# A state-space and FFN block: the scan's output is added to x by TensorE in the bank of y's transposes and copied by ScalarE, and SyncE's transfers are reordered

## The reference

```python
# 1: state-space block over the context, gated by the normalised x
u = silu(conv(in_proj @ ctx) + conv_b)
dt_lo, Bm, Cm = split(x_proj @ u);  delta = softplus(dt_proj @ dt_lo + dt_b)
state = state * exp(delta * A) + (delta * u) * Bm      # 512 steps, 16 states per channel
y = (sum_n state * Cm + D * u) * silu(layernorm(x))
x = x + tanh(g_xattn) * y^T
# 2: feed-forward block on layernorm(x): w1, w2 up (2048), w3 down
h = silu(bit_linear(r, w1, g1)) * bit_linear(r, w2, g2)
x = x + tanh(g_ffn) * bit_linear(h, w3, g3)
# bit_linear: rmsnorm, gain, rounding to 8 bits by the row's maximum, ternary weights
```

## Time and profile before

| | |
|---|---|
| median of the timed runs | 683.2 us |
| the profiled execution | 686.62 us |
| its span, first to last instruction | 684.7 us |
| busy: PE / DVE / ACT / POOL | 608.6 / 603.5 / 555.7 / 548.3 us |
| mean granted TensorE clock | 0.933 |
| DVE, scans of line 1272 | 128, 292.1 us |
| DVE, `add_input` of line 1263 | 128, 157.8 us |

### The profile page before, as it was taken

The page is one execution under the profiler, slowest core; times in us unless marked ns, Lnnn a source line. Parts: engine busy times, 40 slices in busy tenths (PEclk is TensorE's granted clock), DMA queues, the critical chain, the costliest instruction groups (busy, mean ns, idle before and its releaser), DMA issues.

```text
span 684.7 us, 8262 instructions
## 1 busy us (share of the span) xinstructions
PE 608.6 (89%) x2552; PEld 250.0 (37%) x2552; DVE 603.5 (88%) x580; ACT 555.7 (81%) x808; POOL 548.3 (80%) x341
## 2 busy tenths in 40 slices
PE   6987757989789999989999999978898979796997
PEld 3432221535254333423333333332333333332443
DVE  2996988988887899999999999999999999977675
ACT  3658993879679998998989998989889878756874
POOL 5134568995698999999989989998999999977740
PEclk9969777999889999999999999989999999899999
DMA  7699683636942122224412112144212121000000
GB/s 205 241 268 346 213 291 109 215 127 197 248 162 86 47 61 74 66 55 120 103 31 52 46 54 55 54 119 108 63 46 54 39 51 44 15 16 0 17 32 32
DMA packets 40573, 71.25 MB, mean 104 GB/s; under 512 B 10913, under 2 KB 13473, under 8 KB 38481
## 3 DMA queue, kind: packets, MB, share of 16 engines
q1 hardware_dynamic: 37312, 61.28, 31.3%
q10 hardware_dynamic: 3216, 9.44, 4.4%
HBM read 49.46 MB, written 4.46 MB: 79 GB/s over the span
## 4 chain that ended last, share of the span: by engine, by line
PE 30%; DVE 26%; issue 7%; ACT 5%; POOL 2%; DVEq 0%; ACTq 0%; POOLq 0%
DVE hb L1272 14%; PE ring L1700 10%; DVE dbu_ps L1263 6%; PE ring L1802 5%; PE y_ps L1653 5%; PE du_ps L1645 3%; PE ring L1626 2%; PE ring L1765 2%; DVE am L1328 1%; POOL h L682 1%; ACT dA L961 1%; PE ring L1607 1%; DVE h_max L1432 1%; PE ring L1757 1%; DVE fst L1305 1%
## 5 line engine op out<-in xcount | busy, mean ns | idle before, releaser
L1272 DVE TENSOR_TENSOR_SCAN hb<-dA,dbu_ps 128x1024 f32<-128x1024 f32 x128 | 292.1, 2282 | 9.3 <-PE y_ps L1653 1.6
L754 POOL TENSOR_TENSOR hb<-hb,bc_rep 128x2048 f32<-128x2048 f32 x52 | 235.7, 4534 | 34.9 <-DVE hb L1272 29.2
L1263 DVE TENSOR_TENSOR dbu_ps<-du_ps,bc_rep 128x1024 f32<-128x1024 f32 x128 | 157.8, 1232 | 22.1 <-PE du_ps L1645 12.4
L961 ACT ACTIVATE dA<-dl_rep,a_neg 128x511 f32<-128x511 f32 x256 | 163.4, 714 | 9.6 <-DMA dl_rep<-delta 9.1
L1653 PE MATMUL y_ps<-hb,sel_q 128*32 128x512 f32 x496 | 120.0, 629 | 1.3 <-POOL hb L754 1.1
L1645 PE MATMUL du_ps<-du,sel_q 32*128 32x512 f32 x128 | 76.9, 682 | 37.7 <-DVE dbu_ps L1263 37.5
L682 POOL TENSOR_TENSOR h<-h,up_sb 128x1024 f32<-128x1024 f32 x24 | 57.1, 2381 | 12.3 <-ACT up_sb L979 10.7
L1802 PE MATMUL ring<-w3T,hT 128*128 128x512 fp8e4 x256 | 61.2, 386 | 0.9 <-ACT hT L1078 0.4
L675 POOL TENSOR_TENSOR up_sb<-h,g3b 128x1024 f32<-128x1024 f32 x24 | 56.6, 2357 | 1.9
L1653 PEld LDWEIGHTS y_ps<-hb,sel_q 128*32 128x32 f32 x496 | 27.4, 115 | 83.0 <-issue 78.1
L1700 PE MATMUL ring<-w1T,a12T 128*128 128x512 fp8e4 x208 | 53.9, 382 | 1.0 <-ACT hb L971 1.0
(11 more groups left out here) (198 smaller groups left out, 965.9 us busy)
## 6 DMA issues: line engine op xcount, KB each, us to landing
dl_rep<-delta SPq DMA_DIRECT2D x256, 64.0 KB, 2.0
bc_rep<-bc_scratch SPq DMA_DIRECT2D x28, 256.0 KB, 4.8
h<-in_L_ffn_w_dram SPq DMA_DIRECT2D x5, 1024.0 KB, 10.8
x<-in_L_ffn_w_dram SPq DMA_DIRECT2D x5, 1024.0 KB, 8.0
up_sb<-in_L_ffn_w_dram SPq DMA_DIRECT2D x5, 1024.0 KB, 8.2
xt<-in_x_dram SPq DMA_DIRECT2D x16, 256.0 KB, 3.0
out_dram<-x SPq DMA_DIRECT2D x16, 256.0 KB, 2.0
h<-in_L_ffn_w_dram ACTq DMA_DIRECT2D x3, 1024.0 KB, 6.6
```

The source lines that it names most:

```text
L754: g.tensor_tensor(hb[:, s % 4, :, :], hb[:, s % 4, :, :], c_rep(s // 16), ALU.mult)\
L961: ins = a.activation(dA[:, s % 2, i, 1:L], dl[:, 1:L], ACT.Exp, scale=a_neg[:, s % 16, i:i + 1])
L1263: v.tensor_tensor(dbu_ps[:, :, :], du_ps[:, :].unsqueeze(1).to_broadcast([P, 2, L]), b_rep(b)[:, 2 * half:2 * half + 2, :], ALU.mult).then ...
L1272: v.tensor_tensor_scan(hb[:, s % 4, 2 * half:2 * half + 2, :].rearrange("p a l -> p (a l)"), dA[:, s % 2, 2 * half:2 * half + 2, :].rearra ...
```

## The change

- DVE's `add_scan` goes, but for the last one. The gate is multiplied in `gated_y`, whose first call now waits for the gate.
- TensorE, for k < 15, makes each piece of the transpose as a plain product of `yz` with the identity (accumulation begun) and adds a product of the identity with x1's piece in the same bank. It waits for x1's load, which DVE did before. The last block keeps transposes, and DVE adds it (`add_last_scan`).
- ACT copies the bank into x1 (`x1_evac`): at q = 2 ahead of `evac_hT` where k > 4 and not a multiple of 4, else at q = 1.
- SyncE: the loads of chunk 2 and of the last z rows, before at the head of the loop, go behind the delta of step 2 and to s = 6; x1's and ctx's loads go to s = 3 and s = 5; `load_b(b+1)` goes to q = 1, right behind `store_bc(b+1)`.
- DVE's last z statistics spread over s = 5 and 8 to 11 (before 4 to 8), GpSimd's `z_affine(1)` one step later.
- TensorE: `sum_states(2k-1)` ahead of `x_proj`.
- Tail: `h_gain(11, 1)` from GpSimd to DVE (`row_before_tail`), `normalise(13)` behind the first silu, `first_tail_dequant` as two instructions.

```diff
@@ -548,8 +548,6 @@
             bcast_delta(0)
             bcast_delta(1)
             load_c(0)
-            load_chunk(2)
-            load_z(B - 1)
             for k in range(KQ):
                 b, et = divmod(k, ET)
                 for q in range(Q):
@@ -566,14 +564,18 @@
                         next_chunk(c)
                     if s + 2 < Q * KQ:
                         bcast_delta(s + 2)
+                    if s == 0:
+                        load_chunk(2)
                     if s == 1:
                         next_chunk(0)
+                    if s == 6:
+                        load_z(B - 1)
                     if q == 1 and et == ET - 1 and b + 1 < B:
                         store_bc(b + 1)
-                    if q == 2 and et == ET - 1 and b + 1 < B:
                         load_b(b + 1)
                     if s == 2:
                         load_xt(1)
+                    if s == 3:
                         load_x1(0)
                     if s == TERN_AT + 2:
                         sp.wait_ge(at_series, 1)
@@ -583,8 +585,8 @@
                     if s == Q * LAG_F + 2:
                         sp.wait_ge(z_read, KQ)
                         sp.dma_start(g3b[:, :], g3.partition_broadcast(P)).then_inc(ld_g3, 16)
-                    if s == 1 or s == Q * (LAG_G + 1) + 2:
-                        nb = 2 if s == 1 else 3
+                    if s == 5 or s == Q * (LAG_G + 1) + 2:
+                        nb = 2 if s == 5 else 3
                         sp.wait_ge(ctxT_done, 2 * nb)
                         if nb == 3:
                             sp.wait_ge(hss_done, 4)
@@ -805,8 +807,6 @@
                     s = Q * k + q
                     if s >= 1:
                         times_c(s - 1)
-                    if s == 3 * Q:
-                        z_affine(1)
                     if TERN_AT <= s < TERN_AT + WCH:
                         tern(s - TERN_AT)
                     if s == TERN_AT:
@@ -821,6 +821,8 @@
                         hidden_rms(gt)
                     if q == 2 and f >= 0:
                         dequant_scales(f)
+                    if s == 3 * Q + 1:
+                        z_affine(1)
                     if q == 1:
                         if k + 1 < KQ:
                             mul_du(k + 1)
@@ -837,7 +839,6 @@
             pool.wait_ge(a_tail, 2)
             times_up(TAIL - 1, 1)
             row_rstd(TAIL + 1)
-            h_gain(TAIL - 1, 1)
             hidden_rms(TAIL - 1)
             mul_gains(TAIL + 1)
             row_rstd(TAIL + 2)
@@ -1055,6 +1056,13 @@
                 a.activation(delta[:, (KQ - 1) % ND, 0:256].bitcast(BF16), hidden(ft)[:, 512 * c:512 * c + 512], ACT.Square,
                              accum_out=h_ss[:, 2 * c - 3:2 * c - 2]).then_inc(hss_done, 1)
 
+            def x1_evac(k):
+
+                bb, e2 = divmod(k, ET)
+                filled(act, ("yzT", k))
+                a.activation(x1[:, bb % XB, :, P * e2:P * (e2 + 1)], bank(("yzT", k))[:, :].rearrange("p (t e) -> p t e", e=P),
+                             ACT.Copy).then_inc(x1_done, 1)
+
             def square_sum(ft, i):
 
                 if ft < TAIL:
@@ -1084,6 +1092,8 @@
                 for q in range(Q):
                     s = Q * k + q
                     if q == 2:
+                        if k > LAG_F and et:
+                            x1_evac(k - 1)
                         if g >= 0:
                             evac_hT(g, (0, 1))
                     if q == 3 and f >= 0 and by_act(f + 1):
@@ -1114,6 +1124,8 @@
                             normalise(f)
                         if g >= 0:
                             quant_hidden(g)
+                        if k >= 1 and (et == 0 or k < LAG_F):
+                            x1_evac(k - 1)
                         if f >= 0 and f % ET == 0:
                             normalise(f)
                     if q == (1 if k else 2):
@@ -1155,10 +1167,11 @@
             quant(TAIL)
             evac_first_aT(0)
             evac_first_aT(1)
-            normalise(TAIL + 1)
             square_sum(TAIL - 1, 1)
             for ft in range(TAIL, NT):
                 gate_silu(ft, 0)
+                if ft == TAIL:
+                    normalise(ft + 1)
                 if TAIL < ft < NT - 2:
                     normalise(ft + 2)
                 gate_silu(ft, 1)
@@ -1286,18 +1299,13 @@
                 dst = hidden(ft)[:, 512 * c:512 * c + 512]
                 v.scalar_tensor_tensor(dst, bank(job)[:, :], deq[:, ft % 4, 1:2], dst, ALU.mult, ALU.mult).then_inc(h_tail, 1)
 
-            def add_scan(k):
-
+            def add_last_scan():
+
+                k = KQ - 1
                 bb, e2 = divmod(k, ET)
-                job = ("yzT", k)
-                filled(dve, job)
-                if k == 0:
-                    dve.wait_ge(gate_done, 1)
-                if e2 == 0:
-                    dve.wait_ge(ld_x1[bb % XB], 16 if bb < XB else 16 * (1 + ET))
+                filled(dve, ("yzT", k))
                 dst = x1[:, bb % XB, :, P * e2:P * (e2 + 1)]
-                v.scalar_tensor_tensor(dst, bank(job)[:, :].rearrange("p (t e) -> p t e", e=P),
-                                       gates[:, 0:1], dst, ALU.mult, ALU.add).then_inc(x1_done, 1)
+                v.tensor_tensor(dst, bank(("yzT", k))[:, :].rearrange("p (t e) -> p t e", e=P), dst, ALU.add).then_inc(x1_done, 1)
 
             def row_stats(ft):
                 if ft % ET == 0:
@@ -1366,8 +1374,9 @@
 
                 dve.wait_ge(silu_done, 4 * (TAIL - 3))
                 dve.wait_ge(up_done, 4 * (TAIL - 3))
-                v.scalar_tensor_tensor(deq[:, TAIL % 4, :], am[:, :], fsc[:, TAIL % 4, 2:3], alpha[:, 0:2],
-                                       ALU.mult, ALU.mult).then_inc(deq_done, 2)
+                for i in range(2):
+                    v.tensor_scalar(deq[:, TAIL % 4, i:i + 1], am[:, i:i + 1], fsc[:, TAIL % 4, 2:3], alpha[:, i:i + 1],
+                                    ALU.mult, ALU.mult).then_inc(deq_done, 1)
 
             def last_times_c():
 
@@ -1412,7 +1421,9 @@
                 dve.wait_ge(z_done, k + 1)
                 if k >= 1:
                     filled(dve, ("yzT", k - 1))
-                v.tensor_tensor(yz[:, :], y_ps[:, :], xt[:, k % 2, :], ALU.mult).then_inc(yz_done, 1)
+                if k == 0:
+                    dve.wait_ge(gate_done, 1)
+                v.scalar_tensor_tensor(yz[:, :], y_ps[:, :], gates[:, 0:1], xt[:, k % 2, :], ALU.mult, ALU.mult).then_inc(yz_done, 1)
 
             def output(ft):
 
@@ -1432,6 +1443,12 @@
                 return mark(v.tensor_reduce(h_max[:, i:i + 1], gained(ft)[:, H // 2 * i:H // 2 * (i + 1)], AX.X, ALU.max,
                                             apply_absolute_value=True))
 
+            def row_before_tail():
+
+                half = slice(H // 2, H)
+                dve.wait_ge(h_pool, 2 * TAIL)
+                v.tensor_tensor(gained(TAIL - 1)[:, half], hidden(TAIL - 1)[:, half], g3b[:, half], ALU.mult).then_inc(h_mul, 1)
+
             def last_gain(lo, hi):
 
                 dve.wait_ge(h_tail, 4 * (NT - 1 - TAIL) + hi // 512)
@@ -1462,8 +1479,10 @@
                 for q in range(Q):
                     s = Q * k + q
                     add_input(s, 0)
-                    if Q <= s < Q + 5:
-                        z_row_stats(KQ // 2 + 3 + s - Q)
+                    if s == Q + 1:
+                        z_row_stats(KQ // 2 + 3)
+                    if 2 * Q <= s < 3 * Q:
+                        z_row_stats(KQ // 2 + ET + s - 2 * Q)
                     if s == TERN_AT:
                         weight_sums()
                     if q == 1:
@@ -1472,8 +1491,6 @@
                     if q == 2:
                         if f >= 0 and f % ET == 0:
                             row_bias(f)
-                        if k >= 1 and et:
-                            add_scan(k - 1)
                     scan(s, 0)
                     if s == 0:
                         copy_b(2)
@@ -1500,8 +1517,6 @@
                         alpha_large()
                     scan(s, 1)
                     if q == 1:
-                        if k >= 1 and et == 0:
-                            add_scan(k - 1)
                         if f >= 0 and f % ET == 0:
                             link(row_stats(f))
                             link(row_aggr(f))
@@ -1519,7 +1534,7 @@
 
             last_times_c()
             gated_y(KQ - 1)
-            add_scan(KQ - 1)
+            add_last_scan()
             rows(TAIL)
             centred_gain(0)
             first_tail_scale(0)
@@ -1527,8 +1542,9 @@
             first_tail_scale(1)
             first_tail_dequant()
             rows(TAIL + 1)
+            row_before_tail()
+            row_bias(TAIL + 1)
             hidden_max(TAIL - 1, 0)
-            row_bias(TAIL + 1)
             for ft in range(TAIL, NT):
                 if ft == TAIL:
                     mul_up(ft, 0)
@@ -1772,8 +1788,16 @@
                 else:
```

(14 more changed lines are left out.)

## The result

The changed kernel takes 693.5 us in the median (692.9 to 695.06, four runs); the kernel before, run on the same chip, 683.9 us. The ratio is 1.0136, with a 95% interval of 1.0103 to 1.0168: **9.3 us slower** (7.0 to 11.5), and 2.5 us above the upper end of the forecast range. Its profiled execution took 692.9 us with a span of 691.1; against the profiled execution before that is only 6.3 us, because the latter lay 3.4 us above the median of its three runs.

A forecast was written before the change was run, and what follows sets the result against it. DVE sets the scan loop's pace, TensorE level with it from 249.6 to 305.7 us. Terms: -6.0 at k = 4, +8.9 from k = 5, -1.9 tail, together +1.0: 684.2 us, range 677.5 to 691.

The forecast's parts named there:

- the lateness of TensorE: TensorE: 1.5 us more per k, making it 2.7 us late by k=7; cancelled to 0 in k=9, 10, 13, 14.
- k = 5 to 7: DVE waits at k=7 for the late du broadcast, after a margin of 1.1 us: +1.6 us.
- The price of a product: TensorE: eight products are 16 records of 0.125 us, 2.0 us, 1.5 more per k than now (bounds 1.2, 3.2).
- Rival C: A plain product of 128 columns costs load plus pass, 3.2 us more per k: 690.7 us; chance 0.18.
- ACT's copy: Fifteen copies of 0.69 us: free inside k>4; batch borders wait for it and products: +0.1, +1.4, +1.3 (k=4, 8, 12).
- The swap: sum_states ahead of x_proj: -0.8 us at k=3, +2.7 at k=7 (x_proj late for ACT), +1.0 at k=11.
- The start: Loads moved behind step 2's delta end ACT's 7.00 us wait: -3.6 us (0 to -5.45).
- rival D: Memory queues, not the order, set when delta lands; -3.6 and -2.2 shrink to a third: 688.1 us; chance 0.12.
- the sign I named: Start: ACT's wait for delta at step 2 gone, DVE at its fourth step near 60.2 instead of 63.85 us.
- z statistics: Three statistics move from before the weight sums, where hidden by ACT, to after: 3 x 0.45 = +1.3 us.
- load_b: Issued a step earlier, DVE's 2.21 us wait for B's copies goes: -2.2 us (0 if memory queues stay full).
- The tail: h_gain(11, 1) to DVE, normalise(13) behind first silu: nearly all of ACT's 2.13 us wait goes, -1.9 us (0 to -2.1).

The follow-up runs named there:

- sum_only: Kernel before with only the scan's sum made by TensorE products, ACT's copy and the gate in gated_y: 697.07 against 683.03 us, +13.0.
- extra_pe: Kernel before with each transpose of yz written four times for k = 0 to 14, useless TensorE work: 698.28 against 684.77 us, +13.4.
- sum_borders_dve: sum_only with the sums of k = 3, 7, 11 left to transposes and DVE: 693.71 us against 684.90 for the kernel before, +7.3.
- sync_only: Kernel before with only SyncE's transfers reordered and the z statistics and z_affine(1) moved: 676.36 against 683.03 us, -7.4.

## Why the prediction was wrong, point by point

- **The step that failed** is the lateness of TensorE outside k = 5 to 7. What bounds the kernel was read rightly: I had found TensorE full from 249.6 to 305.7 us, and charged lateness in k = 5 to 7, at the borders and at the end. But for k = 2 and 3 I booked DVE's 0.39 us twice (-0.8) on rows of DVE alone, for k = 1 I charged nothing, and for k = 9 and 10 I let the two cancel. From k = 1 to k = 4 the forecast for the scan's sum was thus -0.8 us, and sum_only's scans lost 4.8: 1.1 in k = 1, 1.3 in k = 2, 1.6 at y of k = 3, 0.8 behind it. From k = 8, step 2, to k = 12 it was 0, and sum_only lost 1.4; for k = 13 and 14 zero was right. The rows of sum_only, first k = 2, then k = 3:

```profile
123.76 0.49 PE L1787 MATMUL ring<-ident,yz 128*128 128x128 f32 x2
...
131.77 1.12 PE L1649 MATMUL du_ps<-du,sel_q 32*128 32x512 f32 x2
...
132.93 1.23 DVE L1274 TENSOR_TENSOR dbu_ps<-du_ps,bc_rep 128x1024 f32<-128x1024 f32 x1 [1.64 <-PE du_ps L1649]
...
145.82 1.79 PE L1649 MATMUL du_ps<-du,sel_q 32*128 32x512 f32 x2 [1.85 <-DVE dbu_ps L1274]
147.54 6.29 PE L1621 MATMUL ring<-u,w_xT 128*48 128x512 f32 x8
...
157.43 0.75 DVE L1423 SCALAR_TENSOR_TENSOR yz<-y_ps,gates,xt 128x512 f32<-128x512 f32 x1 [3.82 <-PE y_ps L1657]
```

  and of the kernel before at k = 3:

```profile
143.93 1.09 PE L1645 MATMUL du_ps<-du,sel_q 32*128 32x512 f32 x2 [1.99 <-DVE dbu_ps L1263]
144.95 5.33 PE L1617 MATMUL ring<-u,w_xT 128*48 128x512 f32 x8
```

  TensorE has idle time around k = 2, but not between the products and the du that DVE waits for: already in the kernel before it works from 112.6 to 141.9 us without a pause. So the products' time arrives at DVE. At k = 3 TensorE starts du as soon as DVE lets it, in both kernels, and the products' time is gone; the 1.65 us by which y's wait grows (3.82 for 2.17) are du at 1.79 instead of 1.09 us and x_proj at 6.29 instead of 5.33. That is the slow clock: 0.57 granted from du's start to the sums of y, where it was 0.73 before. extra_pe has the same 0.57, 6.29 and 3.82. At k = 1 the weight sums come late: ACT waits 0.98 us for a convolution that TensorE does behind the products, and 1.61 in extra_pe, which has no copy. What added TensorE time is worth over the whole kernel extra_pe shows: 69%.
- **The price of a product** was right enough: 1.39 us more per k against 1.5. The page's factor of four did not appear. A plain product of 128 columns takes 0.22 us (two records), a transpose in a row of sixteen 0.11: a factor of two. The Trainium skill (TensorE: Matmul & The Clock Gate, Terms) says four, and by it, as an estimate, a k would have cost 3.5 us more; the trace disagrees. Rival C had the wrong mechanism (load plus pass). That its 60% is near the measured 69 is chance, for it was taken of another sum; and its 690.7, the nearest of the four, was reached by a price that this kernel does not pay.
- **ACT's copy** took 0.60 us, and nothing shows that it costs anything in sum_only: at k = 12 and 8 extra_pe is as slow without it, and at k = 1 ACT waits for TensorE behind it. "At k = 4 +0.1, swallowed by the wait for GpSimd" was right: the scans of sum_only lose nothing there. k = 8 was right in size (+1.4 against 1.3 by sum_borders_dve), k = 12 too small (+1.3 against 2.1 to 2.4), and in both the price is TensorE's.
- **k = 5 to 7**: +1.6 forecast, 2.0 in sum_only's scans. Right. **k = 15**: +0.9 forecast; `gated_y(15)` waits 1.0 us longer in sum_only, but from k = 13 to the end it loses only 0.2 by the profiles.
- **The swap**: -0.8, +2.7 and +1.0 forecast (+1.8 at k = 7 where the products are not there to make TensorE late). Alone, k = 3 gives nothing by its scans, k = 7 costs 2.5, k = 11 costs 2.9. At k = 7 ACT's wait was forecast at 3.1 and is 2.96 us, and DVE's `quant_scales` comes late as described. What was missed is that TensorE waits for ACT too, and du comes 1.15 us late behind it; and at k = 11 a loss four k later, whose cause is open. In the changed kernel 7.2 us, not 2.9.
- **The start**: -3.6 forecast; sync_only's scans win 5.8 from the first scan to k = 1 and keep 4.9 behind the weight sums. The mechanism was right, and rival D is out, but the sign I named was not: DVE at its fourth step near 60.2, measured 56.58. (60.23 is the step's second half.) Of the 7.3 us by which that is ahead of 63.85, 2.1 were there at the first scan, 3.6 are TensorE's wait, and 1.6 are the convolutions behind it, 7.01 instead of 8.58 us, as the granted clock of that stretch was 0.83 behind the pause and 1.00 without it. The changed kernel keeps 5.2 us behind the weight sums, or 3.0 from its first scan, which is what ACT's absolute sums allow.
- **z statistics**: +1.3 forecast. sync_only's scans lose 2.7 us in k = 2; three statistics are 1.35 of them, and y's wait there grows from 0.43 to 1.78 us, which no term had.
- **load_b**: -2.2 forecast, 5.0 in the traces and 2.7 to 4.1 in the runs: the chain over GpSimd was not followed.
- **The tail**: -1.9 forecast; 2.0 in the traces, 1.5 by the ratios. Right in size, but ACT's wait isn't gone (1.99 us at 634.19): ACT's earlier work came forward as well.

By parts: forecast -4.5 + 4.5 + 2.9 - 1.9 = +1.0, measured -7.4 + 13.0 + 5.9 - 1.5 = +10.0. All four signs came out as forecast, the tail's by its trace alone. The missing 9.0 us are 8.5 of the scan's sum, 3.0 of the swap and 0.4 of the tail, less 2.9 that the transfers gave more.

## What to carry to other kernels

When two engines run level, don't ask how much idle time the second has, but whether that idle time lies in front of the instruction that the first waits for; the cheapest test is to add useless work to it and measure (here 69% came through, and the same run told the copy's price from the products'). Taking 0.45 us from one engine and giving 1.4 to the other was a loss even at the right price per instruction. Price a pause of TensorE twice: once as a wait, and once for the clock behind it; and look first whether the kernel before has the same slow stretch. And when two timelines are compared, check that the rows are of the same half step: the sign at 60.2 us looked fulfilled, because the second half of the fourth step starts at 60.23.
